# Global attention of an adaLN block: another order of the work of a head pair on three engines, and a third buffer of probabilities

## The chip, the cores and the metric

The kernel runs on one core of one Trainium2 chip. The metric is the time of one execution on the device in microseconds. Lower is better. The core has a matrix engine (TensorE, PE in the profile; its weight loads are PEld), a vector engine (VectorE, DVE), a scalar engine (ScalarE, ACT), GpSimd (POOL) and the queue that issues most DMAs (SyncE, SP). The engines run side by side and wait for one another through semaphores only; each takes its own instructions strictly in the order of the program.

## The reference

A block with two residual branches on x of shape (4, 1024, 256), both modulated from a condition vector. The change touches the first branch only, causal attention with 16 heads of 64:

```python
def proj(W, bias):
    y = jnp.tanh(states @ W + bias)
    return y.reshape(b, s, h, d).transpose(0, 2, 1, 3)
q, k, v = (proj(Wq, bq), proj(Wk, bk), proj(Wv, bv))
alpha = jnp.einsum('bhqd,bhkd->bhqk', q, k) / jnp.sqrt(jnp.float32(d))
alpha = jnp.where(causal, alpha, jnp.finfo(jnp.float32).min)
alpha = jax.nn.softmax(alpha, axis=-1)
ctx = jnp.einsum('bhqk,bhkd->bhqd', alpha, v)
ctx = ctx.transpose(0, 2, 1, 3).reshape(b, s, h * d)
return jnp.tanh(ctx @ Wo + bo)
```

The second branch (two layers of local attention with window 128 and a gated MLP) takes the rest of the time and is the same in both kernels.

## The kernel before

Attention (`phase_attention`) runs over 4 batches of 1024 tokens, and in each over 8 pairs of heads. The loop body holds two pairs, written out. To keep precision, a factor is split into a rounded high part and a remainder (low part), and a product of two factors is three matmuls: high x high, high x low, low x high.

The scores of a pair are cut into 12 units `UNITS` of 128 keys by up to 512 queries, for both heads: 4 for the first half of the queries (`qc` 0), 8 for the second. A unit on the diagonal computes only the queries from `off` on (1024, 768, 512 or 256 columns for the two heads together) and ends with a matmul that adds the causal mask (L561). A unit passes through: `scores` on TensorE (L557, six matmuls, each head on 64 rows of the array) into one of two accumulators `ps_s`; the exponential on ScalarE (L502) into `probs`; on VectorE the cast to the high part (L429) and the remainder (L434); `value_products` on TensorE (L573 to L575, three matmuls for each head and 128 queries) into `ps_o`. `probs`, `p_hi` and `p_lo` have two buffers each. After the units of one half, VectorE takes reciprocals of the row sums and normalises into `ctx_tok` (L400, L402), TensorE transposes it (`context`, L581), ScalarE copies the high part (L482) and VectorE forms the remainder (L408).

Beside it each pair prepares the next one: six projections (`PROJ`: values, queries and keys, in halves of 512 tokens; six matmuls each, L74 to L76, into `ps_m[i % 2]`), each followed on ScalarE by two tanhs (L471 in full precision into `stage`, L473 rounded) and on VectorE by the remainder (L390). The values are transposed on TensorE (`values`, L542), the high part into `ps_m[1]` and the low part into `ps_m[0]`, and copied out by ScalarE (L478) and VectorE (L395). The weights of the pair after next are rounded on ScalarE (L465) and their remainder is taken on VectorE (L382).

The order within a pair is a loop over steps s = 1 to 13 with tables: at step s TensorE computes scores s, then the projection that `PROJ_AT` names, then the transposes of `VALUES_AT`, at step 11 (`CTX_AT`) the context of the first half, and then the value products of unit s - 2 (`LAG`); after the loop, scores 0 of the next pair and the context of the second half. VectorE and ScalarE loop over units and put the other work behind the units of the same tables. At the end of a batch TensorE computes the output projection, which needs the remainders of both contexts.

Of the kernel before, what the change touches and what calls it, by code (L numbers as in the profile page):

```python
# [17 lines left out]
F16 = mybir.dt.float16  # L18
ALU = mybir.AluOpType
# [4 lines left out]
P = 128  # L24
# [5 lines left out]
HP = H // 2  # L30
# [11 lines left out]
def at(n):  # L42
    return n + CREDIT
# [229 lines left out]
LAG = 2  # L273
# [4 lines left out]
PROJ_AT = {1: 0, 2: 1, 6: 2, 7: 3, 9: 4, 10: 5}  # L278
VALUES_AT = {3: 0, 4: 1}
CTX_AT = 11  # L280
ACT_HI = ()
DVE_HI = [u for u in range(NU) if u not in ACT_HI]
NHI = len(DVE_HI)


def phase_attention(nc, io, scr, keep):

    with ExitStack() as ctx:
# [37 lines left out]
        NPAIR = B * HP  # L326

# [3 lines left out]
        with nc.Block() as block:  # L331
# [44 lines left out]
            def _(dve):  # L376
# [20 lines left out]
                def normalise(n, count):  # L397

                    dve.wait_ge(pv_done, at(count))
# [19 lines left out]
                with dve.Fori(0, B) as b:  # L419
                    with dve.Fori(0, HP // 2) as j:  # L420
                        for par in range(2):
                            hp = j * 2 + par
                            it = b * HP + hp
                            for u, (qc, kt) in enumerate(UNITS):
                                off = max(0, kt * P - qc * CH)
                                dve.wait_ge(exp_done, at(it * NU + u + 1))
                                dve.wait_ge(pv_done, at(it * NU + u - 1))
                                if u in DVE_HI:
                                    dve.tensor_copy(p_hi[u % 2][:, :, off:], probs[u % 2][:, :, off:]).then_inc(p_hi_done, 1)  # L429
                                if u == CT - 1 + LAG:  # L430
                                    normalise(it * NC, it * NU + CT)
                                if u in DVE_HI:
                                    dve.wait_ge(p_hi_done, at(it * NHI + DVE_HI.index(u) + 1))
                                dve.tensor_tensor(p_lo[u % 2][:, :, off:], probs[u % 2][:, :, off:],  # L434
                                                  p_hi[u % 2][:, :, off:], ALU.subtract).then_inc(p_lo_done, 1)
                                if u in PROJ_AT:
                                    split_projection(NPJ * (it + 1), PROJ_AT[u], 1 - par)
                                if VALUES_AT.get(u) == 1:
                                    low_values(it + 1, 1 - par)
                                if u == CTX_AT:  # L440
                                    low_context(it * NC, hp, 0)
                            normalise(it * NC + 1, it * NU + NU)
                            split_weights(it + 2)
                            low_context(it * NC + 1, hp, 1)
# [13 lines left out]
            def _(act):  # L458
# [8 lines left out]
                def project(base, i, hp, dst):  # L467
# [3 lines left out]
                    act.activation(stage[:, i % 2, :], ps_m[i % 2][:], ACT.Tanh, bias=bias[:, w, ds(hp, 1)]).then_inc(pj_full, 1)  # L471
                    hi = vT[0] if w == V_ else qk[dst][w - 1][0]
# [13 lines left out]
                for i in range(NPJ):  # L486
                    project(0, i, 0, 0)
# [5 lines left out]
                with act.Fori(0, B) as b:  # L493
                    with act.Fori(0, HP // 2) as j:
                        for par in range(2):
                            hp = j * 2 + par
                            it = b * HP + hp
                            for u, (qc, kt) in enumerate(UNITS):
                                off = max(0, kt * P - qc * CH)
                                act.wait_ge(sc_done, it * NU + u + 1)  # L500
                                act.wait_ge(p_lo_done, at(it * NU + u - 1))
                                step = act.activation(probs[u % 2][:, :, off:], ps_s[u % 2][:, :, off:], ACT.Exp,  # L502
                                                      bias=shift[:], scale=SCORE_SCALE)
                                if u in ACT_HI:
                                    act.wait_ge(pv_done, at(it * NU + u - 1))
                                    step = act.activation(p_hi[u % 2][:, :, off:], ps_s[u % 2][:, :, off:], ACT.Exp,
                                                          bias=shift[:], scale=SCORE_SCALE)
                                step.then_inc(exp_done, 1)
                                if u in PROJ_AT:
                                    project(NPJ * (it + 1), PROJ_AT[u], (hp + 1) % HP, 1 - par)  # L510
# [1108 lines left out]
```

## Time and profile before

| | us |
|---|---|
| median of 3 runs (2948.10 to 2950.08) | 2948.11 |
| the profiled execution | 2949.01 |
| its span, first to last instruction | 2947.2 |
| first to last exponential of attention (L502) | 113.3 to 1145 |
| TensorE busy (matmuls) over the span | 2541.4, 86% |
| VectorE busy | 2056.4, 70% |
| ScalarE busy | 1586.2, 54% |

The profile is of one execution, 1.8 us longer than its span for what lies before the first and after the last instruction. The shares are means over all stages; attention is somewhat over a third of the span. In a timeline a row is an instruction or several of one kind; the number in brackets is the idle time of its engine before it and who ended it.

### The profile page before, as it was taken

The page shows a single profiled execution, that of the slowest core. Times are in us where ns is not written, and L with a number is a line of the kernel's source. Part 1 is how long each engine was busy: PE and PEld are TensorE (multiplying, and loading weights), DVE is VectorE, ACT ScalarE, POOL GpSimd, SP SyncE. Part 2 cuts the span into 40 slices and gives each one's busy share as a digit, 9 for nine tenths or more (in the row PEclk, how much of TensorE's full clock was granted, in tenths as well). Part 3 has the DMA queues.
Part 4 walks back from the last instruction along what each step waited for, and adds up shares of the span by engine and source line. Part 5 has one row for each costly group of instructions (what it writes and reads, how often), then busy time and mean ns, then how long its engine had stood idle before and what let it go on. Part 6 is the DMA issues. An engine that isn't in the chain of part 4 may idle for free. (4 is left out here: it accounts for less than half of the span.)

```text
span 2947.2 us, 65973 instructions
## 1 busy us (share of the span) xinstructions
PE 2541.4 (86%) x21520; PEld 1928.2 (65%) x21520; DVE 2056.4 (70%) x4571; ACT 1586.2 (54%) x3034; POOL 528.7 (18%) x534
## 2 busy tenths in 40 slices
PE   5699989989998998199999995899799999994996
PEld 3466656666666666177777774788577777773885
DVE  5588778858885885667777774566567777773656
ACT  2577567646764674356656654333466565652332
POOL 0000000000000000333343342111233433431111
PEclk7899999999999999599999998899899999996998
DMA  4400020010002000400000000100100000000003
GB/s 148 154 11 16 6 73 12 15 65 12 16 11 69 11 16 17 146 1 0 7 2 5 4 3 7 45 0 0 34 0 7 0 7 0 7 0 7 0 0 114
DMA packets 74545, 77.25 MB, mean 26 GB/s; under 512 B 4224, under 2 KB 67320, under 8 KB 72952
## 3 DMA queue, kind: packets, MB, share of 16 engines
q1 hardware_dynamic: 74488, 76.46, 7.9%
q8 instruction: 40, 0.66, 0.1%
q14 instruction: 17, 0.14, 0.0%
HBM read 55.48 MB, written 16.78 MB: 25 GB/s over the span
## 5 line engine op out<-in xcount | busy, mean ns | idle before, releaser
L502 ACT ACTIVATE at_p<-at_ps_s,at_shift 128x1024 f32<-128x1024 f32 (+3 forms) x384 | 342.9, 901 | 91.6 <-PE at_ps_s L561 39.9
L434 DVE TENSOR_TENSOR at_p_lo<-at_p,at_p_hi 128x1024 f16<-128x1024 f32 (+3 forms) x384 | 367.9, 958 | 12.1
L1023 ACT ACTIVATE ly_probs<-ly_masked,ly_small,ly_rq 128x256 f32<-128x256 f32 x512 | 302.3, 592 | 63.9 <-DVE ly_small L1206 63.2
L74 PE MATMUL ly_ps<-ly_w_hi,ly_operands 128*128 128x512 f32 (+1 forms) x792 | 293.7, 371 | 15.6 <-DVE ly_operands L1156 9.0
L429 DVE CAST at_p_hi<-at_p 128x1024 f16<-128x1024 f32 (+3 forms) x384 | 213.8, 557 | 94.8 <-PE at_ps_o L575 52.6
L75 PE MATMUL ly_ps<-ly_w_lo,ly_operands 128*128 128x512 f32 (+1 forms) x792 | 273.4, 345 | 0.0
L76 PE MATMUL ly_ps<-ly_w_hi,ly_operands 128*128 128x512 f32 (+1 forms) x792 | 273.1, 345 | 0.0
L573 PE MATMUL at_ps_o<-at_v,at_p_hi 128*128 128x65 f16 x2304 | 248.9, 194 | 24.3 <-DVE at_p_lo L434 24.3
L1409 PEld LDWEIGHTS ly_ps<-ly_values,ly_probs_T 128*128 128x128 f32 x2048 | 258.9, 192 | 15.6 <-issue 0.4
L573 PEld LDWEIGHTS at_ps_o<-at_v,at_p_hi 128*128 128x128 f16 x2304 | 209.9, 96 | 85.1 <-DVE at_p_lo L434 44.3
L1409 PE MATMUL ly_ps<-ly_values,ly_probs_T 128*128 x2048 | 260.1, 270 | 0.0
L574 PE MATMUL at_ps_o<-at_v,at_p_hi 128*128 128x64 f16 x2304 | 247.3, 194 | 0.0
L575 PE MATMUL at_ps_o<-at_v,at_p_lo 128*128 128x65 f16 x2304 | 245.7, 192 | 0.0
L1032 ACT ACTIVATE ly_probs_T<-ly_ps 128x512 f32<-128x512 f32 x256 | 150.3, 587 | 167.1 <-PE ly_ps L1409 150.1
L1389 PE MATMUL ly_ps<-ly_operands_plain 64*128 64x256 f32 x1040 | 183.7, 430 | 50.9 <-DVE ly_small L1203 50.9
L74 PE MATMUL at_ps_m<-at_hT,at_w_hi 128*128 (+1 forms) x396 | 177.0, 447 | 57.2 <-DVE at_v L395 37.2
L1203 DVE CUSTOM_DVE_ANT_0 ly_masked<-ly_ps,ly_mask 128x256 f32<-128x256 f32 x520 | 198.4, 419 | 25.4 <-DVE ly_mask L1303 11.7
L575 PEld LDWEIGHTS at_ps_o<-at_v,at_p_lo 128*128 128x128 f16 x2304 | 213.5, 99 | 0.0
L574 PEld LDWEIGHTS at_ps_o<-at_v,at_p_hi 128*128 128x128 f16 x2304 | 213.1, 97 | 0.4
L1055 ACT ACTIVATE ly_probs<-ly_ps,ly_b 128x512 f32<-128x512 f32 x96 | 66.3, 690 | 256.1 <-PE ly_ps L76 256.1
L471 ACT ACTIVATE at_stage<-at_ps_m,at_bias 128x512 f32<-128x512 f32 x198 | 136.1, 687 | 118.0 <-PE at_ps_m L76 100.4
L905 POOL MEMSET ly_expo<- 128x8 f32 x1 | 0.1, 104 | 1095.3 <-POOLq L331 1095.3
(209 smaller groups left out, 6343.9 us busy)
## 6 DMA issues: line engine op xcount, KB each, us to landing
at_hT<-hT_hi SPq DMA_DIRECT2D x5, 1024.0 KB, 5.2
at_hT<-hT_lo SPq DMA_DIRECT2D x5, 1024.0 KB, 7.7
at_w_raw<-in_Wv SPq DMA_DIRECT2D x34, 128.0 KB, 2.1
at_w_raw<-in_Wq SPq DMA_DIRECT2D x34, 128.0 KB, 2.3
at_w_raw<-in_Wk SPq DMA_DIRECT2D x34, 128.0 KB, 2.3
n_x<-in_states SPq DMA_DIRECT2D x4, 1024.0 KB, 11.6
hT_hi<-n_hi SPq DMA_DIRECT2D x8, 512.0 KB, 3.0
hT_lo<-n_lo SPq DMA_DIRECT2D x8, 512.0 KB, 3.1
```

The lines of the kernel that those rows point to most:

```text
L74: pe.matmul(out, w_hi, x_hi, start=first, stop=False, skip_group_check=True)
L75: pe.matmul(out, w_hi, x_lo, start=False, stop=False, skip_group_check=True)
L76: return pe.matmul(out, w_lo, x_hi, start=False, stop=last, skip_group_check=True)
L429: dve.tensor_copy(p_hi[u % 2][:, :, off:], probs[u % 2][:, :, off:]).then_inc(p_hi_done, 1)
L434: dve.tensor_tensor(p_lo[u % 2][:, :, off:], probs[u % 2][:, :, off:], p_hi[u % 2][:, :, off:], ALU.subtract).then_inc(p_lo_done, 1)
L502: step = act.activation(probs[u % 2][:, :, off:], ps_s[u % 2][:, :, off:], ACT.Exp, bias=shift[:], scale=SCORE_SCALE)
L573: pe.matmul(out, ph, ones_hi, start=(kt == 0 and t == 0), stop=False, skip_group_check=True)
L574: pe.matmul(out[:, 0:DH], ph, lo, start=False, stop=False, skip_group_check=True)
L575: step = pe.matmul(out, pl, ones_hi, start=False, stop=(kt == qc * CT + t), skip_group_check=True)
L1023: step = act.activation(pr[:, j % 2, h, :], sm[:, j % 2, h, :], ACT.Exp, bias=small[:, j % 2, 1, h:h + 1], scale=rq[:, par, 2 * j + h:2 * ...
L1203: dve.tensor_tensor_reduce(sm[:, j % 2, h, :], ps_s[h][:, 0:2 * P], mask[:, par].rearrange("p a b -> p (a b)"), 1.0, -3.0e38, ALU.add, ALU ...
L1409: step = pe.matmul(ps_pv[:, cols], pT[:, (2 * slot + h) * P:(2 * slot + h + 1) * P], vv[:, v_slots[slot], cols], start=(j == 0 and h == 0 ...
```

## The change

The loops and tables are replaced by an order that is written out for each engine, with one helper for each step. The probabilities and both their parts get three buffers (`P_RING`), so that the waits of the casts, the exponentials and the buffers' indices go by 3 where they went by 2. TensorE computes scores 2 and 3, 4 and 5, 6 and 7, 8 and 9, 10 and 11 one after the other. VectorE casts units 2, 6 and 10 before the remainders of 1, 5 and 9, and unit 4 before the copy of the values and the normalisation of the first half. The context of the first half moves behind value product 11; the normalisation of the second half waits until that context has been transposed. The remainders of context 0 and of the last projection stand on VectorE behind the second normalisation and the weights. The waits that stood in TensorE's loop are in the helpers `project`, `scores` and `value_products`, with the same conditions. The number of instructions of each kind with work is the same, and the DMAs are the same. The removed loops stand in the kernel above; of the diff the parts that carry the order:

```diff
-LAG = 2
 V_, Q_, K_ = range(3)
 PROJ = [(V_, 0), (V_, 1), (Q_, 0), (K_, 0), (Q_, 1), (K_, 1)]
 NPJ = len(PROJ)
 FIRST_PROJ = 4
-PROJ_AT = {1: 0, 2: 1, 6: 2, 7: 3, 9: 4, 10: 5}
-VALUES_AT = {3: 0, 4: 1}
-CTX_AT = 11
-ACT_HI = ()
-DVE_HI = [u for u in range(NU) if u not in ACT_HI]
-NHI = len(DVE_HI)
+P_RING = 3
+NQKV_FREE = (NPJ - 1, NPJ)
...
-        probs = [a.sb(f"at_p{i}", [P, 2, CH]) for i in range(2)]
-        p_hi = [a.sb(f"at_p_hi{i}", [P, 2, CH], F16) for i in range(2)]
-        p_lo = [a.sb(f"at_p_lo{i}", [P, 2, CH], F16) for i in range(2)]
+        probs = [a.sb(f"at_p{i}", [P, 2, CH]) for i in range(P_RING)]
+        p_hi = [a.sb(f"at_p_hi{i}", [P, 2, CH], F16) for i in range(P_RING)]
+        p_lo = [a.sb(f"at_p_lo{i}", [P, 2, CH], F16) for i in range(P_RING)]
...
+                def high_probs(it, u):
+                    off = unit_offset(u)
+                    dve.wait_ge(exp_done, at(it * NU + u + 1))
+                    dve.wait_ge(pv_done, at(it * NU + u + 1 - P_RING))
+                    dve.tensor_copy(p_hi[u % P_RING][:, :, off:], probs[u % P_RING][:, :, off:]).then_inc(p_hi_done, 1)
+
+                def low_probs(it, u):
+                    off = unit_offset(u)
+                    dve.wait_ge(p_hi_done, at(it * NU + u + 1))
+                    dve.tensor_tensor(p_lo[u % P_RING][:, :, off:], probs[u % P_RING][:, :, off:],
+                                      p_hi[u % P_RING][:, :, off:], ALU.subtract).then_inc(p_lo_done, 1)
+
+                def reciprocals(it, c):
+                    dve.wait_ge(pv_done, at(it * NU + (CT, NU)[c]))
                     dve.reciprocal(rsum[:], o_view()[:, :, :, DH]).then_inc(r_done, 1)
+
+                def normalise(it, c):
+                    n = it * NC + c
                     dve.wait_ge(r_done, at(n + 1))
+                    if c == 1:
+                        dve.wait_ge(ct_mm, n)
...
+                            ahead, dst = NPJ * (it + 1), 1 - par
+                            high_probs(it, 0)
+                            low_probs(it, 0)
+                            high_probs(it, 1)
+                            high_probs(it, 2)
+                            low_probs(it, 1)
+                            low_probs(it, 2)
+                            split_projection(ahead, 0, dst)
+                            split_projection(ahead, 1, dst)
+                            high_probs(it, 3)
+                            low_probs(it, 3)
+                            high_probs(it, 4)
+                            low_values(it + 1, dst)
+                            reciprocals(it, 0)
+                            low_probs(it, 4)
+                            normalise(it, 0)
+                            high_probs(it, 5)
+                            high_probs(it, 6)
+                            low_probs(it, 5)
+                            low_probs(it, 6)
+                            high_probs(it, 7)
+                            low_probs(it, 7)
+                            high_probs(it, 8)
+                            low_probs(it, 8)
+                            split_projection(ahead, 2, dst)
+                            high_probs(it, 9)
+                            high_probs(it, 10)
+                            low_probs(it, 9)
+                            low_probs(it, 10)
+                            high_probs(it, 11)
+                            low_probs(it, 11)
+                            split_projection(ahead, 3, dst)
+                            split_projection(ahead, 4, dst)
+                            reciprocals(it, 1)
+                            normalise(it, 1)
                             split_weights(it + 2)
+                            low_context(it * NC, hp, 0)
+                            split_projection(ahead, 5, dst)
...
+                def exps(it, u):
+                    off = unit_offset(u)
+                    act.wait_ge(sc_done, it * NU + u + 1)
+                    act.wait_ge(p_lo_done, at(it * NU + u + 1 - P_RING))
+                    act.activation(probs[u % P_RING][:, :, off:], ps_s[u % 2][:, :, off:], ACT.Exp,
+                                   bias=shift[:], scale=SCORE_SCALE).then_inc(exp_done, 1)
...
+                            ahead, then, dst = NPJ * (it + 1), (hp + 1) % HP, 1 - par
+                            exps(it, 0)
+                            exps(it, 1)
+                            tanh_full(ahead, 0, then)
+                            exps(it, 2)
+                            tanh_hi(ahead, 0, then, dst)
+                            exps(it, 3)
+                            tanh_full(ahead, 1, then)
+                            tanh_hi(ahead, 1, then, dst)
+                            exps(it, 4)
+                            exps(it, 5)
+                            exps(it, 6)
+                            high_values(it + 1, dst)
+                            tanh_full(ahead, 2, then)
+                            tanh_hi(ahead, 2, then, dst)
+                            exps(it, 7)
+                            tanh_full(ahead, 3, then)
+                            exps(it, 8)
+                            exps(it, 9)
+                            tanh_hi(ahead, 3, then, dst)
+                            exps(it, 10)
+                            tanh_full(ahead, 4, then)
+                            exps(it, 11)
+                            tanh_hi(ahead, 4, then, dst)
+                            split_weights(it + 2)
+                            tanh_full(ahead, 5, then)
+                            tanh_hi(ahead, 5, then, dst)
+                            high_context(it * NC, hp, 0)
                             high_context(it * NC + 1, hp, 1)
...
+                    n = it * NC + c
+                    pe.wait_ge(pj_hi, at(NPJ * (it + 1) + NQKV_FREE[c]))
...
+                            buf = ((it + 1) // HP) % 2
+                            ahead = NPJ * (it + 1)
+                            scores(b, it, par, 1)
+                            project(it, 0, buf)
+                            scores(b, it, par, 2)
+                            scores(b, it, par, 3)
+                            project(it, 1, buf)
+                            value_products(b, it, par, 0)
+                            scores(b, it, par, 4)
+                            scores(b, it, par, 5)
+                            values(0, ahead)
+                            value_products(b, it, par, 1)
+                            values(1, ahead)
+                            value_products(b, it, par, 2)
+                            value_products(b, it, par, 3)
+                            scores(b, it, par, 6)
+                            scores(b, it, par, 7)
+                            project(it, 2, buf)
+                            value_products(b, it, par, 4)
+                            project(it, 3, buf)
+                            scores(b, it, par, 8)
+                            scores(b, it, par, 9)
+                            value_products(b, it, par, 5)
+                            value_products(b, it, par, 6)
+                            scores(b, it, par, 10)
+                            scores(b, it, par, 11)
+                            value_products(b, it, par, 7)
+                            project(it, 4, buf)
+                            value_products(b, it, par, 8)
+                            project(it, 5, buf)
+                            value_products(b, it, par, 9)
+                            value_products(b, it, par, 10)
+                            value_products(b, it, par, 11)
+                            context(it, 0)
+                            scores(b, it + 1, 1 - par, 0)
+                            context(it, 1)
```

## Rows read from the trace of the kernel before

**Rows 1.** ScalarE's timeline, weight roundings of pairs 9 and 16: start us, us, instruction

```profile
406.13 0.83 ACT L465 ACTIVATE at_w_hi<-at_w_raw 128x768 fp32r<-128x768 f32 x1
...
612.38 0.85 ACT L465 ACTIVATE at_w_hi<-at_w_raw 128x768 fp32r<-128x768 f32 x1
```

**Rows 2.** Busy time in one pair: stretch, length, engines, TensorE clock, DMA share, GB/s

```profile
407.00:436.40 29.40, 27.08 (x364) 18.39 (x364) 25.60 (x40) 20.72 (x29) 0.00 (x0) 1.00 0.05 15
```

**Rows 3.** Waits, 116 to 1150 us: engine <- releaser: us in total, times, longest

```profile
PE at_ps_m L74 <- DVE at_v L395: 37.2, 32, 1.2
...
PE at_ps_m L542 <- ACT at_vT_hi L473: 9.3, 32, 0.4
```

**Rows 4.** TensorE's timeline where it waits: start us, us, instruction, [idle before <- releaser]

```profile
406.81 0.19 PE L575 MATMUL at_ps_o<-at_v,at_p_lo 128*128 128x65 f16 x1
...
407.72 0.20 PE L573 MATMUL at_ps_o<-at_v,at_p_hi 128*128 128x65 f16 x1 [0.72 <-DVE at_p_lo L434]
...
408.77 0.28 PE L561 MATMUL at_ps_s<-at_causal,at_ident 128*128 128x128 f16 x2
...
409.20 0.66 PE L581 MATMUL at_ps_m<-ident,at_ctx_tok 128*128 128x128 f32 x4 [0.15 <-DVE at_ctx_tok L402]
...
409.79 0.34 PE L557 MATMUL at_ps_s<-at_q1hi,at_k1hi 64*128 64x384 f16 x2
...
419.99 0.38 PE L557 MATMUL at_ps_s<-at_q1hi,at_k1lo 64*128 64x512 f16 x2
...
421.53 0.50 PE L74 MATMUL at_ps_m<-at_hT,at_w_hi 128*128 x1 [1.16 <-DVE at_v L395]
```

**Rows 5.** TensorE's timeline, borders between groups without a wait

```profile
405.35 0.28 PE L561 MATMUL at_ps_s<-at_causal,at_ident 128*128 128x128 f16 x2
...
405.47 0.61 PE L581 MATMUL at_ps_m<-ident,at_ctx_tok 128*128 128x128 f32 x4
...
407.86 0.19 PE L574 MATMUL at_ps_o<-at_v,at_p_hi 128*128 128x64 f16 x1
...
407.88 0.20 PE L575 MATMUL at_ps_o<-at_v,at_p_lo 128*128 128x65 f16 x1
...
408.01 0.39 PE L557 MATMUL at_ps_s<-at_q1hi,at_k1hi 64*128 64x512 f16 x2
...
418.51 0.39 PE L557 MATMUL at_ps_s<-at_q1hi,at_k1hi 64*128 64x512 f16 x2
...
424.09 0.38 PE L557 MATMUL at_ps_s<-at_q1lo,at_k1hi 64*128 64x512 f16 x2
...
424.31 0.38 PE L557 MATMUL at_ps_s<-at_q1hi,at_k1lo 64*128 64x512 f16 x2
...
424.62 0.50 PE L74 MATMUL at_ps_m<-at_hT,at_w_hi 128*128 x1
```

**Rows 6.** VectorE's timeline: neighbours that depend and that do not

```profile
409.06 0.95 DVE L382 TENSOR_TENSOR at_w_lo<-at_w_raw,at_w_hi 128x768 fp32r<-128x768 f32 x1
...
411.78 0.69 DVE L429 CAST at_p_hi<-at_p 128x1024 f16<-128x1024 f32 x1 [0.27 <-ACT at_p L502]
...
412.51 1.23 DVE L434 TENSOR_TENSOR at_p_lo<-at_p,at_p_hi 128x1024 f16<-128x1024 f32 x1
...
421.40 0.68 DVE L429 CAST at_p_hi<-at_p 128x1024 f16<-128x1024 f32 x1
...
422.00 0.20 DVE L400 RECIPROCAL at_rsum<-at_ps_o 128x8 f32<-128x8 f32 x1
```

**Rows 7.** ScalarE's timeline: context copy, exponential, tanh after their matmuls

```profile
410.06 0.60 ACT L482 ACTIVATE at_cT_hi<-at_ps_m 128x512 f32 x1 [2.61 <-PE at_ps_m L581]
...
419.45 1.11 ACT L502 ACTIVATE at_p<-at_ps_s,at_shift 128x1024 f32<-128x1024 f32 x1 [0.56 <-PE at_ps_s L557]
...
426.50 0.69 ACT L471 ACTIVATE at_stage<-at_ps_m,at_bias 128x512 f32<-128x512 f32 x1 [0.57 <-PE at_ps_m L76]
```

More of the change, by code:

```diff
@@ L423, in _ @@
                             it = b * HP + hp
[L424 to L441, printed above, removed]
@@ L497, in _ @@
                             it = b * HP + hp
[L498 to L510, printed above, removed]
-                                if VALUES_AT.get(u) == 0:
-                                    high_values(it + 1, 1 - par)
-                                if u == CTX_AT:
-                                    split_weights(it + 2)
-                                    high_context(it * NC, hp, 0)
@@ L527, in _, with project, projection @@
                     pe.sem_inc(s, CREDIT)
-                def project(i, buf):
+                def project(it, i, buf):
+                    base = NPJ * (it + 1)
+                    if i == 0:
+                        pe.wait_ge(ld_hT, 32 * ((it + 1) // HP) + 32)
+                        pe.wait_ge(wl_done, at(it + 2))
+                        pe.wait_ge(vt_lo, at(it + 1))
+                        pe.wait_ge(ct_lo, at(NC * it - 1))
+                    elif i == 1:
+                        pe.wait_ge(vt_hi, at(it + 1))
+                        pe.wait_ge(ct_lo, at(NC * it))
+                    elif i == 2:
+                        pe.wait_ge(vt_lo, at(it + 2))
+                    elif i == 3:
+                        pe.wait_ge(vt_hi, at(it + 2))
+                    else:
+                        pe.wait_ge(pj_hi, at(base + i - 1))
+                    projection(i, buf)
+                def projection(i, buf):
                     w, c = PROJ[i]
@@ L544, in values, with scores, unit_scores @@
                     step.then_inc(vt_mm, 1)
-                def scores(par, u):
+                def scores(b, it, par, u):
+                    if u == 1:
+                        pe.wait_ge(x1_done, at(b * NC - 1))
+                    pe.wait_ge(pj_lo, at(NPJ * it + (FIRST_PROJ if u < CT else NPJ)))
+                    pe.wait_ge(exp_done, at(it * NU + u - 1))
+                    unit_scores(par, u)
+                def unit_scores(par, u):
                     qc, kt = UNITS[u]
@@ L576, in value_products, with context @@
                     step.then_inc(pv_done, 1)
-                def context(n, c):
+                def context(it, c):
+                    n = it * NC + c
+                    pe.wait_ge(pj_hi, at(NPJ * (it + 1) + NQKV_FREE[c]))
                     pe.wait_ge(cx_done, at(n + 1))
@@ L598, in _ @@
                         pe.wait_ge(pj_hi, at(i - 1))
-                    project(i, 0)
+                    projection(i, 0)
                 pe.wait_ge(ld_const, 16 * 4)
@@ L604, in _ @@
                 pe.wait_ge(pj_lo, at(FIRST_PROJ))
-                scores(0, 0)
+                unit_scores(0, 0)
                 with pe.Fori(0, B) as b:
```

74 lines of the change are left out of this document (18 added, 56 removed).

## The prediction

> **What bounds the kernel now.** I read the views in this order: busy shares of one pair of heads, the length of a pair, the waits by engine, then the TensorE timeline of one pair. The change touches one stage only, the loop over 32 pairs in attention. From the weight rounding of pair 9 to that of pair 16, seven pairs take 612.38 - 406.13 = 206.25 us, 29.46 us each [rows 1]; 32 of them are 943 us of the 2947.2 us span. In one pair of 29.40 us TensorE is busy 27.08 us, VectorE 25.60, ScalarE 20.72, and the granted clock is 1.00, the upper level [rows 2]. No engine is full, so the order decides. Among the waits one recurs in all 32 pairs: a projection that waits for VectorE's copy of the values' low part, 37.2 us in all; the values' transposes wait 9.3 us in all, 0.29 per pair [rows 3].
>
> The idle figures understate what TensorE loses, since matmul ends are modelled and overlap, so I count from start to start. Projection 2 starts 421.53 - 419.99 = 1.54 after the last score matmul, where a projection normally follows after 0.31: 1.23 lost. Value product 11 starts 0.91 after the last matmul of product 10, where 0.03 is normal: 0.88 lost. The second context starts 0.43 after the mask matmul, where another first context needs 0.12: 0.31 lost [rows 4, 5]. With the transposes' 0.29 that is 2.71 us per pair in which TensorE waits, and 29.40 - 2.71 = 26.69 us of work. TensorE's work is the next limit.
>
> I weigh a rule of the Trainium skill here (Perfetto Trace Analysis, Identifying the Most-Contended Engine): matmul busy time says little about the room left, the share of weight loads is to be taken. By the loads' 18.39 us [rows 2] 11 us per pair would be free. The borders between groups in the timeline leave no such room, so my sum does not use it.
>
> **The change part by part.** I write S for scores, E for the exponential, H for the cast (high part), L for the remainder, PV for value products, P for projections, C for contexts.
>
> *Two scores together.* Scores use half the rows of the array. A matmul of another shape after them, or they after another, starts late: product to product 0.03, product to scores 0.13; scores to scores 0.22, scores to projection 0.31 [rows 5]. So a switch costs about 0.10. Only S4-S5 and S6-S7 really join; units 2, 8 and 10 end in a mask matmul of the full shape, so S2-S3, S8-S9, S10-S11 still switch. Two fewer runs of scores are four fewer switches: 26.69 - 0.40 = 26.29. Borders that the trace of before lacks, a product straight before a projection or transposes (five per pair), I take at the 0.03 between products; at 0.10 (the nearest switch) they add up to 0.4.
>
> *Casts ahead of remainders.* A cast of 1024 columns takes 0.69 and its own remainder starts 0.73 after it, an independent instruction 0.60 after it [rows 6]: 0.13 per parted couple. Seven of twelve are parted (units 1, 2, 4, 5, 6, 9, 10); one was so before (unit 5). Six times 0.13 is 0.8 us of VectorE per pair. This is off the path once TensorE is full; it makes margin. A rule speaks against it (the Trainium skill, VectorE: DVE Perf Modes, The DRAIN you can't avoid): the next VectorE instruction waits for the pipeline to empty, and a semaphore between them costs nothing extra. By that the 0.8 us would not come; the row of this trace shows 0.13 and decides.
>
> *Third buffer.* The wait before a cast falls from PV two units back to three, likewise the exponential's on the remainder. No instruction is added, the DMAs and the sync queue are unchanged.
>
> *The order.* I walked one pair, t = 0 at P0, with starts from rows: E begins 0.94 after S of a full unit and takes 1.11; a tanh begins 1.88 after its projection and the second some 0.6 later [rows 5, 7]; products take 0.03 per matmul (24 in a full unit), a full score unit 0.65 to 0.75, a projection 1.5. The places where TensorE could wait come out as (ready / wanted): PV0 3.1 / 4.0; P2, the old 1.23 us stall, 8.6 / 9.7, because the copy now needs only S4, S5, PV1 and V1 ahead of it and two more products stand before P2; P3 (needs the copy of the high values) 11.3 / 12.0; S9 (needs E7, which stands behind both tanhs of P2) 13.9 / 14.4; S11 17 / 17.6; PV8 18.1 / 19.8; PV9 20.3 / 22.0; PV11, the old 0.88 stall, 22.1 / 22.9. V0, the old 0.29 stall, 5.7 / 6.2. All waits of before go; the thinnest margin is 0.5.
>
> *The turn of the pair, where a wait is added.* Context 0 moves from the middle to behind PV11, and the second normalisation must now wait until C0 has read the tile that it overwrites. With PV11 starting at x: C0 at x + 0.19, done by 0.86 later (context to copy, 409.20 to 410.06 [rows 4, 7]), so the normalisation starts at x + 1.05. Behind it in VectorE's queue stand the weight remainder (0.60 later, as between the independent neighbours above, 0.95 long) and the context remainder (0.86 after that, 0.69 long: neighbours overlap by 0.09, as 422.00 stands to 421.40 + 0.69 [rows 6]), which ends at x + 3.20. P0 of the next pair waits for both, x + 3.26. TensorE itself gets there at 0.19 + 0.59 (C0 then scores, [rows 4]) + 0.88 (S0: 0.76 to its mask, 0.12 from there) + 0.59 (C1) + 0.69 (S1, three matmuls of 384 columns where S0 has 512) = x + 2.94. So **0.32 us** of new wait. Queued behind P0 are S2 and everything else. S3, which needs E1, would be the next late one: it is ready within 0.3 of its turn.
>
> Sum per pair: 26.29 + 0.32 = 26.61, against 29.46: 2.85 less. Over 32 pairs 91 us. At the end of each of four batches the output projection needs the context remainder of half 0, which was long ready and now ends 1.46 after the normalisation, 0.06 before TensorE starts on it, where C1 alone would let it start after 0.06 + 0.59: about 0.9 us each, 3.6 in all. Net 87 us. The profiled execution lasted 2949.0 us, 0.9 above the median of 2948.1: 2949.0 - 87 = 2862, in terms of the median **2861 us**, 3.0% faster.
>
> **Bounds.** Lower: the turn costs nothing and the unpriced borders nothing, 26.29 per pair: 2949.0 - 101.4 + 3.6 = 2851; the same with the five borders a little cheaper than I took, and product-to-product joins at 0.03 throughout (the walk's own sum is 25.9): 2839. Upper: the five borders at 0.10, 27.0: 2949.0 - 78.7 + 3.6 = 2874. If also VectorE gains nothing from parted casts and its waits in order add the 0.8: 27.8, 2900.
>
> **The rivals.**
> *TensorE is full without a turn wait* (C0 is done sooner than 0.86): about 2847. For it: 0.86 includes ScalarE's start. Against: VectorE's queue behind it is real.
> *VectorE or the hops between engines bind.* VectorE has 24.8 us of its own and some 1.6 us of waits in my walk, so it is within 0.3 us of the pair's length; ten waits with margins of 0.5 to 1 leave little for an exponential late by one tanh (0.6). Half the gain is lost: 2949 - 45 + 3 = 2906. For it: the queues are strictly in order, the exponentials E7, E8, E11 stand behind tanhs that wait for projections. Against: each has a margin in the walk. The drain rule above, as a mechanism of this kernel, ends here too: 0.8 us of VectorE per pair comes back, 26 us, 2887.
> *The change does not do what it says*: with masks between them most pairs of scores join nothing, and only the moved waits matter. That is in my sum for three of five; if the joined ones save nothing either, 26.61 becomes 27.0: 2874.
> *Slower, the ring at the turn.* One mechanism: E11 waits in ScalarE's queue behind the first tanh of P4, so L11, PV11, C0, normalisation, weight remainder, context remainder and P0 form one chain over three engines, where before only C1 hung on the normalisation. It decides from the point where L11 comes more than 0.86 + 2.85 = 3.7 us later than I walked; each microsecond beyond is 32 us. At 5 us late: 2949 + 32 x 1.3 + 4 = about 2994. Against it: P4 is ready early (tanh 2 at 13, wanted at 18.3).
> *The clock* stays at 1.00 in the pair of before [rows 2]; a fuller TensorE gives no reason to fall.
>
> **How the numbers follow.** Forecast (2845 to 2882): 0.70. No turn wait at all, under 2845: 0.06. VectorE or hops bind, 2882 to 2940: 0.15. Within 0.2% (2942 to 2954, about what a measurement of this kernel can tell from no change): 0.04. Slower, by the ring: 0.05. The range takes the forecast and the near half of its neighbours: 2843 to 2898. Faster 0.91, same 0.04, slower 0.05.
>
> **What would show it.** Right: weight roundings 26.6 us apart; the projection's wait for the low values gone from the list of waits; TensorE waiting mainly at P0 for the context remainder, some 0.2 to 0.4 us per pair; 0.22 between the last matmul of S4 and the first of S5. Wrong: new TensorE waits for an exponential before S9, S11 or S3, or for a remainder before a product; VectorE without gaps; a granted clock under 1.00 in the pairs; a second context far behind S0.

## The result and the profile after

| | us |
|---|---|
| median of 4 runs (2852.89 to 2854.50) | 2853.82 |
| the kernel before, same chip, median of 4 | 2948.11 |
| ratio, 95% interval | 0.9679, 0.9662 to 0.9696 |
| the profiled execution's span (before: 2947.2) | 2851.5 |

The kernel is 94.3 us or 3.2% faster; 2861 us was forecast. Busy time, share of the span and instructions of each engine after:

```profile
PE 2513.0 (88%) x21520; PEld 1919.4 (67%) x21520; DVE 2027.5 (71%) x4571; ACT 1570.5 (55%) x3034; POOL 529.3 (19%) x534
```

The length of a pair, read as in [rows 1] from ScalarE's weight rounding, seven pairs apart (start us, us, instruction, idle before it):

```profile
380.17 0.84 ACT L498 ACTIVATE at_w_hi<-at_w_raw 128x768 fp32r<-128x768 f32 x1 [0.55 <-PE at_ps_m L76]
...
565.30 0.84 ACT L498 ACTIVATE at_w_hi<-at_w_raw 128x768 fp32r<-128x768 f32 x1 [0.56 <-PE at_ps_m L76]
```

(565.30 - 380.17) / 7 = 26.45 us, 3.01 less than before; 26.61 was forecast. One pair of it, to compare with [rows 2] (stretch, length, busy time of TensorE, its weight loads, VectorE, ScalarE, GpSimd, then the granted clock):

```profile
433.08:459.51 26.43, 26.29 (x370) 18.19 (x367) 24.73 (x39) 20.22 (x28) 0.00 (x0) 1.00 0.05 15
```

TensorE is busy for 26.29 of 26.43 us where it was 27.08 of 29.40, at the same clock. The waits of [rows 3] are gone from the list of waits. The first line below is the only wait of TensorE for another engine that recurs in every pair there (us in total, times, longest). The second is the wait that the change adds on VectorE. The wait before projection 0, shown further down, is not named in this list: it is booked there as the engine's own issue time.

```profile
PEld at_ps_o L660 <- DVE at_p_lo L405: 8.7, 32, 0.3
DVE at_ctx_tok L417 <- PE at_ps_m L670: 8.3, 32, 0.3
```

Borders inside a pair, TensorE's timeline. First the last matmul of scores 4 and the first of scores 5 (0.22 apart), then the last of value product 4 and the first of projection 3 (0.03 apart, the border that I had no row for; value product 11 to context 0 is 0.03 too):

```profile
442.26 0.38 PE L636 MATMUL at_ps_s<-at_q1hi,at_k1lo 64*128 64x512 f16 x2
...
442.48 0.38 PE L636 MATMUL at_ps_s<-at_q1hi,at_k1hi 64*128 64x512 f16 x2
...
448.94 0.19 PE L662 MATMUL at_ps_o<-at_v,at_p_lo 128*128 128x65 f16 x1
...
448.97 0.47 PE L74 MATMUL at_ps_m<-at_hT,at_w_hi 128*128 x1
```

The turn of the pair, TensorE: context 1, scores 1, its mask and projection 0, first from the first pair of the loop body to the second, then across the end of the loop body:

```profile
435.35 0.52 PE L670 MATMUL at_ps_m<-ident,at_ctx_tok 128*128 128x128 f32 x3
...
435.91 0.34 PE L636 MATMUL at_ps_s<-at_q1hi,at_k1hi 64*128 64x384 f16 x2
...
436.50 0.28 PE L640 MATMUL at_ps_s<-at_causal,at_ident 128*128 128x128 f16 x2
...
436.93 0.49 PE L74 MATMUL at_ps_m<-at_hT,at_w_hi 128*128 x1
...
461.78 0.52 PE L670 MATMUL at_ps_m<-ident,at_ctx_tok 128*128 128x128 f32 x3
...
462.55 0.34 PE L636 MATMUL at_ps_s<-at_q0hi,at_k0hi 64*128 64x384 f16 x2
...
463.14 0.28 PE L640 MATMUL at_ps_s<-at_causal,at_ident 128*128 128x128 f16 x2
...
463.36 0.49 PE L74 MATMUL at_ps_m<-at_hT,at_w_hi 128*128 x1
```

and VectorE at the first of these turns: reciprocal, normalisation, weight remainder, remainder of context 0:

```profile
434.11 0.21 DVE L410 RECIPROCAL at_rsum<-at_ps_o 128x8 f32<-128x8 f32 x1 [0.16 <-PE at_ps_o L662]
...
434.57 0.69 DVE L417 TENSOR_TENSOR at_ctx_tok<-at_ps_o,at_rsum 128x512 f32<-128x512 f32 x1 [0.26 <-PE at_ps_m L670]
...
435.18 0.95 DVE L381 TENSOR_TENSOR at_w_lo<-at_w_raw,at_w_hi 128x768 fp32r<-128x768 f32 x1
...
436.05 0.68 DVE L423 TENSOR_TENSOR at_cT_lo<-at_ps_m,at_cT_hi 128x512 f32 x1
```

A projection normally follows a mask after 0.10. Here projection 0 starts 0.43 after it, 0.33 late: the remainder of context 0 ends at 436.05 + 0.68 = 436.73. The walk had said 0.32. Across the end of the loop body the second context takes 0.77 to the next scores instead of 0.56 (0.21 of loop edge, which the walk did not have). Projection 0 then starts 0.22 after the mask, a wait of only 0.12: TensorE comes to it later, while the chain on VectorE is as long as at the other turn.

### The profile page after: what moved, and what is told of

The parts are those of the page before. It is cut to its first block and busy times, and to the rows that moved or that the text cites. A ratio compares the mean times of both kernels' runs of the same rounds, so it can differ in the third digit from the quotient of the medians.

```text
span 2851.5 us, 65989 instructions
## 1 busy us (share of the span) xinstructions
PE 2513.0 (88%) x21520; PEld 1919.4 (67%) x21520; DVE 2027.5 (71%) x4571; ACT 1570.5 (55%) x3034; POOL 529.3 (19%) x534
## 5 line engine op out<-in xcount | busy, mean ns | idle before, releaser
L504 ACT ACTIVATE at_p<-at_ps_s,at_shift 128x1024 f32<-128x1024 f32 (+3 forms) x384 | 336.0, 900 | 85.2 <-PE at_ps_s L636 45.5
L405 DVE TENSOR_TENSOR at_p_lo<-at_p,at_p_hi 128x1024 f16<-128x1024 f32 (+3 forms) x384 | 357.2, 951 | 5.5
L400 DVE CAST at_p_hi<-at_p 128x1024 f16<-128x1024 f32 (+3 forms) x384 | 206.1, 556 | 51.5 <-ACT at_p L504 26.1
L660 PE MATMUL at_ps_o<-at_v,at_p_hi 128*128 128x65 f16 x2304 | 237.7, 193 | 0.5 <-DVE at_p_lo L405 0.5
L661 PE MATMUL at_ps_o<-at_v,at_p_hi 128*128 128x64 f16 x2304 | 236.9, 194 | 0.0
L662 PE MATMUL at_ps_o<-at_v,at_p_lo 128*128 128x65 f16 x2304 | 235.8, 192 | 0.0
L74 PEld LDWEIGHTS ly_ps<-ly_w_hi,ly_operands 128*128 128x128 f32 x792 | 152.9, 193 | 57.1 <-issue 24.7
L1017 POOL TENSOR_TENSOR ly_rope_a<-ly_rope_a,ly_rope_t 128x512 f32<-128x512 f32 x132 | 176.0, 1334 | 76.0 <-DVE ly_rope_t L1253 76.0
```

Of the source, the lines that this page charges most:

```text
L74: pe.matmul(out, w_hi, x_hi, start=first, stop=False, skip_group_check=True)
L400: dve.tensor_copy(p_hi[u % P_RING][:, :, off:], probs[u % P_RING][:, :, off:]).then_inc(p_hi_done, 1)
L405: dve.tensor_tensor(p_lo[u % P_RING][:, :, off:], probs[u % P_RING][:, :, off:], p_hi[u % P_RING][:, :, off:], ALU.subtract).then_inc(p_lo ...
L504: act.activation(probs[u % P_RING][:, :, off:], ps_s[u % 2][:, :, off:], ACT.Exp, bias=shift[:], scale=SCORE_SCALE).then_inc(exp_done, 1)
L660: pe.matmul(out, ph, ones_hi, start=(kt == 0 and t == 0), stop=False, skip_group_check=True)
L661: pe.matmul(out[:, 0:DH], ph, lo, start=False, stop=False, skip_group_check=True)
```

## The experiments

Each ratio compares a run with the kernel before on the same chip. "After" is the changed kernel, 2853.8 us; it did not run beside the experiments, and the kernel before had medians of 2948.1 to 2949.7 us beside them. So a difference to after in microseconds is uncertain by 1 to 2 us, and where it is small the length of a pair from the trace says more. In the expectations, Theory A is the explanation that I held, Rival B and C are others with their own times.

### Two buffers of probabilities in the new order

```diff
-P_RING = 3
+P_RING = 2
```

> The changed kernel with two buffers of probabilities instead of three, order untouched. Theory A (the new order needs the third buffer): the casts of units 2, 6 and 10, which now stand ahead of the remainders of 1, 5 and 9, must wait for value products 0, 4 and 8, and the remainders, the projection remainders, V1 and S5 queue behind them; by the timeline of the changed kernel 3 to 5 us per pair are lost, 2950 to 3010 us, that is no faster than the kernel before. Rival B (the buffer is margin only): 2854 to 2860 us.

Measured: 3092.3 us, ratio 1.048 (1.047 to 1.050). The direction is Theory A's; its size is missed. 3 to 5 us per pair were expected, the pair is 34.17 us, 7.7 more than after. Waits over the loop:

```profile
ACT at_p L504 <- DVE at_p_lo L405: 311.5, 253, 2.8
DVE at_p_hi L400 <- PE at_ps_o L662: 264.6, 206, 4.9
PEld at_ps_s L636 <- ACT at_p L504: 142.1, 128, 1.8
```

A ring: the exponential waits for a remainder, which stands behind a cast that waits for a value product, which stands in TensorE's queue behind scores that wait for an exponential. I had counted the delays at three places and not their way round the ring.

TensorE's clock falls as well. Scores 11 start 1.95 us after the mask before them, and about a microsecond later the granted clock falls to 0.50, the lower level, for 3 us in the pair looked at. Below are the late scores, then the stretch behind them as in [rows 2]:

```profile
471.20 0.23 PE L636 MATMUL at_ps_s<-at_q1hi,at_k1hi 64*128 64x128 f16 x2 [1.67 <-ACT at_p L504]
...
472.46:475.46 3.00, 3.00 (x17) 2.09 (x17) 0.69 (x2) 0.56 (x2) 0.00 (x0) 0.50 0.03 5
```

Projection 4 takes 2.13 us from its first to its last matmul there (1.24 after), and value product 8 takes 1.18 (0.71 after), 1.4 us together. From 400 to 600 us the mean granted clock is 0.95, against 1.00 in the kernel before and 0.99 after. How much of the 7.7 us goes by the clock in all is not shown.

### Two buffers, the casts in couples again

```diff
-P_RING = 3
+P_RING = 2
...
-                            high_probs(it, 2)
                             low_probs(it, 1)
+                            high_probs(it, 2)
                             low_probs(it, 2)
```

(and likewise for units 5 and 6, 9 and 10)

> The changed kernel with two buffers of probabilities and with the casts of units 2, 6 and 10 behind the remainders of 1, 5 and 9. With two buffers and the casts ahead the time was 3092 us; with three buffers and this order of casts 2853 us. Theory A (two buffers fail because the casts ahead block VectorE): most of the loss goes, 2880 us or less. Rival B (two buffers fail because the paired scores let the value products lag by three to four units): at least half of the loss stays, 2960 us or more.

Measured: 2988.6 us, 1.014 (1.012 to 1.015). Rival B: of the 238 us that two buffers cost with the casts ahead, 135 remain without (2988.6 against 2853.3 with three buffers). The same two waits lead the list, smaller:

```profile
ACT at_p L504 <- DVE at_p_lo L405: 196.1, 205, 2.4
DVE at_p_hi L400 <- PE at_ps_o L662: 146.4, 147, 3.9
```

The granted clock is 1.00 here (450.60 to 481.20 us), so the clock may be part of what the couples gave back. The rest of the order needs the third buffer too; that it is the products' longer lag behind paired scores is argued from the order, not shown.

### Three buffers, the casts in couples again

The edit on the casts shown above, alone; `P_RING` stays 3.

> The changed kernel with the casts of units 2, 6 and 10 right behind the remainders of 1, 5 and 9, in couples as before. Each parted couple costs 0.13 us of VectorE; six couples are joined again, 0.8 us of VectorE per pair. Theory A (TensorE is full, VectorE has margin): 2854 to 2858 us. Rival B (VectorE is close to the bound): up to 0.8 us per pair, 2879 us. If the couple costs nothing at all, VectorE's timeline shows 0.60 between a cast and its own remainder.

Measured: 2853.3 us, 0.9677 (0.9663 to 0.9690), the same as after. Theory A: the casts ahead of remainders are worth nothing here. VectorE of this kernel, cast 8 and its remainder, then cast 4 and the independent copy behind it:

```profile
452.37 0.69 DVE L400 CAST at_p_hi<-at_p 128x1024 f16<-128x1024 f32 x1
...
453.10 1.22 DVE L405 TENSOR_TENSOR at_p_lo<-at_p,at_p_hi 128x1024 f16<-128x1024 f32 x1
...
443.65 0.69 DVE L400 CAST at_p_hi<-at_p 128x1024 f16<-128x1024 f32 x1 [0.25 <-PE at_ps_o L662]
...
444.26 0.69 DVE L394 COPY at_v<-at_ps_m 128x1024 f16<-128x1024 f16 x1
```

0.73 and 0.61: a couple does cost 0.12 to 0.13 more, and VectorE has room for it. Before cast 4 it is idle for 0.25 us here; after, with the casts parted:

```profile
444.50 0.69 DVE L400 CAST at_p_hi<-at_p 128x1024 f16<-128x1024 f32 x1 [0.46 <-PE at_ps_o L662]
```

it is idle 0.46 at that place: the time won was spent waiting.

### The third buffer alone, in the kernel before

```diff
-        probs = [a.sb(f"at_p{i}", [P, 2, CH]) for i in range(2)]
+        probs = [a.sb(f"at_p{i}", [P, 2, CH]) for i in range(3)]
...
-                                dve.wait_ge(pv_done, at(it * NU + u - 1))
+                                dve.wait_ge(pv_done, at(it * NU + u - 2))
```

(the same for `p_hi`, `p_lo`, the exponential's wait and the indices)

> The kernel before with three buffers of probabilities, its order untouched. Theory A (order and buffer belong together): only the casts that waited for value products come earlier, by 0.7 us before product 11, so its stall of 0.88 us shrinks to about 0.1; the stall of 1.23 us before projection 2 hangs on the exponential of unit 4 and stays: 22 to 28 us gained, 2920 to 2926 us. Rival B (the third buffer carries most of the gain): 2870 to 2890 us.

Measured: 2946.3 us, 0.9988 (0.9979 to 0.9998). Neither: next to nothing. The stall before value product 11 shrank (idle 0.26 us instead of 0.72), as Theory A says in direction, but the second context now starts 0.90 after the mask where it was 0.43 [rows 4], and that takes it all back:

```profile
491.84 0.20 PE L573 MATMUL at_ps_o<-at_v,at_p_hi 128*128 128x65 f16 x1 [0.26 <-DVE at_p_lo L434]
...
492.88 0.29 PE L561 MATMUL at_ps_s<-at_causal,at_ident 128*128 128x128 f16 x2
...
493.78 0.55 PE L581 MATMUL at_ps_m<-ident,at_ctx_tok 128*128 128x128 f32 x3 [0.61 <-DVE at_ctx_tok L402]
```

The reciprocal stands in VectorE's queue behind the remainder of context 0, which waits for ScalarE's copy. I had stopped the walk one wait too early.

### The copy of the low values ahead of remainder 4, in the kernel before

```diff
+                                if VALUES_AT.get(u) == 1:
+                                    low_values(it + 1, 1 - par)
                                 if u in DVE_HI:
                                     dve.wait_ge(p_hi_done, ...
...
-                                if VALUES_AT.get(u) == 1:
-                                    low_values(it + 1, 1 - par)
```

> The kernel before with one change: VectorE copies the low part of the values before remainder 4 instead of behind it. Projection 2, which waited 1.23 us in each pair for that copy, finds it done. Theory A (a wait takes its place): behind the copy remainder 4, cast 5 and the first normalisation are as late as before, and value product 4 waits for the normalisation, about 1 us; 0.2 us per pair is gained, 2942 us. Rival B (that stall was the path): 1.2 us per pair, 2910 us.

Measured: 2942.9 us, 0.9978 (0.9969 to 0.9988). Theory A. The largest stall of before, 1.23 us per pair, is gone from the list of waits, and value product 4 right behind that projection waits instead (TensorE's timeline, last matmul of projection 2 and the next one, 1.28 apart where 0.24 is normal; then the list of waits):

```profile
448.74 0.39 PE L76 MATMUL at_ps_m<-at_hT,at_w_lo 128*128 x1
...
450.02 0.20 PE L573 MATMUL at_ps_o<-at_v,at_p_hi 128*128 128x65 f16 x1 [0.90 <-DVE at_ctx_tok L402]
```

```profile
PE at_ps_o L573 <- DVE at_ctx_tok L402: 28.6, 32, 0.9
```

### Both single cures together, in the kernel before

(the two edits above together)

> The kernel before with both three buffers of probabilities and the copy of the low values ahead of remainder 4. With three buffers alone the stall before value product 11 had gone and 0.8 us stood before the second context instead. Theory A (each cure only moves its wait while the order stays): value product 4 and the second context wait instead, 2935 to 2945 us. Rival B (with both cures the gains show): 2910 us or less.

Measured: 2940.0 us, 0.9975 (0.9964 to 0.9985), Theory A:

```profile
PE at_ps_o L573 <- DVE at_ctx_tok L402: 28.0, 32, 0.9
...
PE at_ps_m L581 <- DVE at_ctx_tok L402: 19.6, 32, 0.6
```

Both waits stand where the cured ones had been pushed to, each in all 32 pairs. In the new order they are gone from the list together. Which of its moves are needed for that is not shown: no run lies between this one and the full order.

### Four more switches

```diff
+                            scores(b, it, par, 4)
                             value_products(b, it, par, 0)
-                            scores(b, it, par, 4)
                             scores(b, it, par, 5)
```

(and value product 3 between scores 6 and 7; a switch is a change between matmuls of 64 and of 128 rows)

> The changed kernel with value product 0 moved between scores 4 and 5, and value product 3 between scores 6 and 7: four more changes between matmuls of 64 and of 128 rows per pair, the same matmuls, waits still met. Theory A (a switch costs 0.10 us of TensorE): 0.4 us per pair, 13 us, 2867 us. Rival B (the switch is hidden, the gain is all from removed waits): 2854 us.

Measured: 2868.5 us, 0.9724 (0.9711 to 0.9738); 14.7 us over after, Theory A. The pair is 26.86 us against 26.45, 0.41 for four switches (13 us over 32 pairs): 0.10 each, as the rows of before gave it.

### A second buffer for the normalised context

```diff
-        ctx_tok = a.sb("at_ctx_tok", [P, CT, 2, DH])
+        ctx_tok = [a.sb(f"at_ctx_tok{i}", [P, CT, 2, DH]) for i in range(NC)]
...
-                    if c == 1:
-                        dve.wait_ge(ct_mm, n)
```

(and `ctx_tok[c]` where `ctx_tok` was read and written)

> The changed kernel with two buffers for the normalised context, so that the second normalisation does not wait until context 0 is transposed. Theory A (the chain context 0, normalisation, weight remainder, context remainder, projection 0 sets the turn of the pair): the normalisation starts 0.23 us earlier and projection 0 with it: 7 us, 2846.5 us. Rival B (projection 0 waits for something else, or only for its own row of waits to be read): 2854 us.

Measured: 2845.7 us, 0.9652 (0.9639 to 0.9665); 8.1 us below after, Theory A. The pair is 26.22 us, 0.22 less. Projection 0 follows the mask after 0.22 instead of 0.43; across the end of the loop body it follows after 0.10 instead of 0.22, and there the context is followed by scores 1 after 0.68 instead of 0.77. The first of these turns:

```profile
435.30 0.28 PE L638 MATMUL at_ps_s<-at_causal,at_ident 128*128 128x128 f16 x2
...
435.52 0.49 PE L74 MATMUL at_ps_m<-at_hT,at_w_hi 128*128 x1
```

### The weight remainder in two parts

```diff
+                            split_value_weights(it + 2)
                             reciprocals(it, 1)
                             normalise(it, 1)
-                            split_weights(it + 2)
                             low_context(it * NC, hp, 0)
+                            split_qk_weights()
...
-                        pe.wait_ge(wl_done, at(it + 2))
+                        pe.wait_ge(wv_done, at(it + 2))
```

(projection 2 waits for `wl_done`)

> The changed kernel with the weight remainder taken in two parts: that of the value weights ahead of the second reciprocal, where VectorE is idle for 0.16 and 0.26 us, that of query and key weights behind the remainder of context 0. Projection 0 then needs only work that ends 0.87 us earlier. Theory A (the 0.33 us before projection 0 are that chain): the wait goes, 32 x 0.33 = 10.6 us, and at the four batch ends 0.8 us each: 2840 to 2843 us. Rival B (part of the 0.33 is the cost of four waits in a row on TensorE): some 0.15 us stays, 2848 us.

Measured: 2844.9 us, 0.9650 (0.9637 to 0.9663); 8.9 us below after, between the two. Projection 0 follows the mask after 0.10, the normal distance, so the wait was the chain and not the reading of the waits:

```profile
432.95 0.28 PE L649 MATMUL at_ps_s<-at_causal,at_ident 128*128 128x128 f16 x2
...
433.05 0.48 PE L74 MATMUL at_ps_m<-at_hT,at_w_hi 128*128 x1
...
457.92 0.55 PE L679 MATMUL at_ps_m<-ident,at_ctx_tok 128*128 128x128 f32 x3
...
458.67 0.34 PE L645 MATMUL at_ps_s<-at_q0hi,at_k0hi 64*128 64x384 f16 x2
```

The second couple of rows shows what is left: context 1 to scores 1 across the end of the loop body, 0.75 instead of 0.56. Pairs alternate between 26.16 and 26.33 us, 26.24 on average. Every second turn had only 0.12 to give, not 0.33; the average of 0.22 times 32 is 7.2 us. At each of the four batch ends the wait for the remainder of context 0 falls from 0.8 to 0.4, which is about the rest.

### Masks together

```diff
-                            scores(b, it, par, 2)
-                            scores(b, it, par, 3)
+                            scores(b, it, par, 2, False)
+                            scores(b, it, par, 3, False)
+                            unit_masks(2, 3)
```

(and for 8 and 9, 10 and 11; on top of the kernel with the remainder in two parts)

> The changed kernel with the weight remainder in two parts (as in e5_wsplit) and, for units 2 and 3, 8 and 9, 10 and 11, both mask matmuls behind both units' score matmuls, so that those pairs of scores really join. Six switches less per pair of heads. Theory A (TensorE is full and a switch costs 0.10 to 0.115 us): 0.6 to 0.7 us per pair, 19 to 22 us below e5_wsplit's 2845, less up to 3 us for exponential 9, which comes later and is wanted by scores 11: 2823 to 2829 us. Rival B (the price is in the change of accumulator or in the mask, not in the switch of shape): 2843 us. Rival C (the later ends of units 2, 8 and 10 open waits for exponentials): over 2835 us, with waits of scores on the exponential in the list.

Measured: 2836.9 us, 0.9618 (0.9605 to 0.9631), the fastest kernel of this study; 8.0 us below the one it builds on (9 by the pair, 25.96 us against 26.24), half or less of what Theory A gave, more than Rival B's 2. Borders between the two units of scores, 8 to 9 and 10 to 11, and the wait of the weight loads:

```profile
446.78 0.38 PE L654 MATMUL at_ps_s<-at_q1hi,at_k1lo 64*128 64x512 f16 x2
...
446.99 0.33 PE L654 MATMUL at_ps_s<-at_q1hi,at_k1hi 64*128 64x384 f16 x2
...
449.59 0.27 PE L654 MATMUL at_ps_s<-at_q1hi,at_k1lo 64*128 64x256 f16 x2
...
449.94 0.23 PE L654 MATMUL at_ps_s<-at_q1hi,at_k1hi 64*128 64x128 f16 x2
```

```profile
PEld at_ps_s L654 <- ACT at_p L512: 24.7, 78, 0.7
```

Scores 8 and 9 join at 0.21, and from scores 8 to value product 5 it takes 1.48 us (446.33 to 447.81) against 1.69. Scores 11 start 0.35 after the last matmul of scores 10 where matmuls of that size stand 0.11 apart, and no time is won there: they wait for exponential 9, which now ends later. Scores 3 start 0.23 after scores 2 where 0.11 is normal: without the mask between them their turn comes before exponential 1 has ended. So a clean join gives 0.21 for two switches, which fits the 0.10 each, and two of the three joins open a wait. That is Rival C, in its mechanism and in its time of over 2835 us.

## Why the prediction was right

The time came out 7 us below the forecast, inside the range, and by the mechanism that was forecast: TensorE's waits go, its work is the limit, and a wait for the context remainder appears before projection 0. Some of the terms were off.

**What bounds it.** After, a pair is 26.45 us. Without the average wait of 0.22 before projection 0 and half a loop edge of 0.21, TensorE's work is about 26.1. The forecast for the work was 26.29. The 0.16 between is a wait of before that I sized too small. I counted the other three stalls from start to start, but for the transposes of the values I took the idle figure, 0.29. From start to start they stand 0.57 after the mask in front of them:

```profile
415.17 0.28 PE L561 MATMUL at_ps_s<-at_causal,at_ident 128*128 128x128 f16 x2
...
415.74 0.62 PE L542 MATMUL at_ps_m<-at_ident,at_vT_hi 128*128 128x128 f16 x8 [0.28 <-ACT at_vT_hi L473]
```

A context follows a mask after 0.12 [rows 5], so 0.45 was lost there, 0.16 more than 0.29. With it the waits of before are 2.87 us per pair and not 2.71, and 29.40 - 2.87 - 0.40 gives 26.13. The busy share of [rows 2] would have allowed only 29.40 - 27.08 = 2.3 us per pair, less than the 3.01 that came.

**Switches.** 0.10 each, shown by adding four. Only scores 4 and 5 and scores 6 and 7 join, as forecast, so of the 94 us about 13 are theirs.

**Casts ahead.** Off the path, as forecast, and shown: 2853.3 against 2853.8 us. VectorE's busy time in a pair did fall, from 25.60 to 24.73 us, where 0.8 less was forecast. The page VectorE: DVE Perf Modes of the Trainium skill (The DRAIN you can't avoid) says of a chain of copies that a semaphore after each costs nothing extra, and that an instruction that is not held starts before the pipeline is empty. The 0.61 of an independent instruction behind a cast of 0.69 agrees with the second. The first does not carry over to this kernel: a cast's own remainder, which waits for the cast's semaphore, starts after 0.73, and the trace decides, though no run's time hangs on it.

**Third buffer.** The prediction treated it as a wait that moves and gave no price to its absence. That is the gap in it: alone it brings 0.1%, and without it the new order is 4.8% slower than the kernel before. The rest of the order and the buffer are worth something only together.

**Which stalls go.** The forecast that all of them go and that none but the turn takes their place held; the single cures show how little that follows from removing one. In the kernel before each cured stall came back in full or nearly so within the same pair.

**The turn.** 0.32 was forecast and 0.33 found at one turn of two; at the other it was 0.12 plus 0.21 of loop edge. The chain through the second normalisation, weight remainder and context remainder is shown by the two runs that shorten it (second buffer, split remainder), 8.1 and 8.9 us faster. That 0.32 meets 0.33 so closely is partly luck. Value product 11 starts at 433.72 before the first turn shown above. From there the walk has the normalisation at 434.77 and it starts at 434.57. The walk has the remainder ending at 436.92, and it ends at 436.73. The walk has projection 0 start 0.06 behind that end, and it starts 0.20 behind. These errors cancel.

**Batch ends.** TensorE waits for the remainder of context 0 before the output projection:

```profile
PE at_ps_s L74 <- DVE at_cT_lo L423: 3.2, 4, 0.8
```

Each is 0.8 us by the idle figure; at the first batch end the projection starts 1.44 after the second context where it was 0.56 in before, 0.88 more. 0.9 was forecast. But the interval across a batch end lost only 0.25 us on average (0.22 at the first), and what gave the rest back can be seen at the first one. In the first pair of a new batch projection 0 has no wait, where other pairs have 0.22 on average. And the granted clock, which is 0.50 after the pause between batches in both kernels, is back at 1.00 before projection 1 now, while it came back within projection 1 in before. Stretch of projection 1, before and then after, as in [rows 2]:

```profile
382.72:384.63 1.91, 1.91 (x9) 1.38 (x7) 0.69 (x1) 1.29 (x3) 0.00 (x0) 0.76 0.23 34
...
360.18:361.63 1.45, 1.45 (x8) 1.02 (x7) 0.83 (x2) 1.45 (x3) 0.00 (x0) 1.00 0.39 56
```

That is 0.46 us. Only this batch end was followed so.

**The sum.** 28 pairs inside batches x 3.01 = 84.3 us. The remaining four intervals, across three batch ends and at the start, shorten by 2.7 to 2.9 us each. Together they are 95.5 us of the spans' 95.7; what lies before the loop is 1.0 us longer and what lies behind it 1.0 us shorter, so these cancel. Between the profiled executions the forecast was 8 us short (7 between the medians): 5 are the 0.16 us of work per pair, and 2 to 3 are the batch ends at 0.25 each instead of 0.9.

## What to carry to other kernels

Count a full engine from start to start over one period, and walk a new order to its end with the durations of the old one: that gave the length of the pair to 0.6%. Count every stall in the same way: one idle figure among the distances from start to start hid 5 us of the gain. Removing one stall in a loop with strictly ordered queues says little about the path; the next wait in the same queue takes its place, and even two cures together gave 0.3% where the whole order gave 3.2%. Price the absence of each buffer too: with one buffer fewer the good order was the slowest kernel of all, and TensorE's clock fell in it as well.

## What the runs showed of the hardware

Around the end of the loop body TensorE's second context is followed by scores 1 after 0.67 us in the kernel before, 0.77 after, 0.68 with two context buffers and 0.75 with the remainder in two parts, where the other turn has 0.54 to 0.59: the edge costs 0.1 to 0.2 us. A matmul of the full shape costs nothing extra at the border from value products to a projection or transpose (0.03), while a change between 64 and 128 rows costs 0.10, shown by adding four per pair. The page TensorEngine Tiling (Array Packing) of the Trainium skill (Key Properties) says that a change of tiling mode drains the engine; the runs agree in that a change costs time, and put it at 0.10 us.

The granted clock is 1.00 in the pairs of both kernels. In attention it was seen at 0.50, the lower of the two levels, in two places: behind the pause of some 4 us between two batches, and in the order with two buffers behind the wait of 1.95 us before scores 11.
